# Group-norm statistics of y: small VectorE operations with one operand in PSUM, copies behind them, slot zero's a step later

## The reference, cut to what matters

```python
# x, ctx: (8, 512, 2048); Wt, Wp, Wg: (512, 512); Wz: (512, 64), 8 groups of 64 channels
q = layernorm(x)
t = Wt @ ctx; p = Wp @ q; g = Wg @ ctx              # per batch element
att = sum over (64 channels, 2048) of p * g          # one number per group
y = Wz_group @ (att * t)                             # per group
mu, var = mean and variance of y over (64 channels, 2048), per group
yn = (y - mu) * rsqrt(var + 1e-5)
x = x + (yn * gn_w + gn_b + ctx)
x = x + FFN(layernorm(x))     # 16 heads of 128 features, permuted: up 128x512, gelu, down 512x128
```

## Time and profile before

| what | us |
|---|---|
| median of 3 runs (lowest, highest) | 1515.17 (1512.41, 1517.02) |
| the profiled execution's own time | 1520.61 |
| its span, first to last instruction | 1518.8 |
| TensorE busy in it | 1496.8 |
| VectorE, ScalarE, GpSimd busy | 1201.1, 1065.3, 967.8 |
| granted TensorE clock | 1.00 of full speed |

### The profile page before, as it was taken

One profiled execution on the slowest core, in us unless ns is written; L12 is line 12 of the kernel. 1 busy time (PEld: TensorE's weight loads), 2 busy tenths in 40 slices (PEclk: granted clock), 3 DMA queues, 4 the chain that ended last, 5 costly groups with the idle time before them and its releaser, 6 DMA issues.

```text
span 1518.8 us, 19146 instructions
## 1 busy us (share of the span) xinstructions
PE 1496.8 (99%) x6592; PEld 1231.6 (81%) x6592; DVE 1201.1 (79%) x1514; ACT 1065.3 (70%) x1321; POOL 967.8 (64%) x765
## 2 busy tenths in 40 slices
PE   8999999999999999999999999999999999999998
PEld 7878887887878888888888888888888888877786
DVE  4999868887778767887778877887678876889786
ACT  4636757855778568784687847877478783899786
POOL 1673685298862668525794357835589264888787
PEclk9999999999999999999999999999999999999999
DMA  9998797786667937778376774767748676758886
GB/s 330 329 375 332 230 312 281 270 267 210 226 238 267 286 110 223 253 256 266 125 250 243 250 248 140 266 240 249 215 151 281 250 235 186 259 193 261 272 275 223
DMA packets 166865, 374.76 MB, mean 247 GB/s; under 512 B 14960, under 2 KB 80496, under 8 KB 158576
## 3 DMA queue, kind: packets, MB, share of 16 engines
q1 hardware_dynamic: 141424, 281.25, 56.3%
q0 software_dynamic: 25344, 92.29, 17.1%
HBM read 287.45 MB, written 86.03 MB: 246 GB/s over the span
## 4 chain that ended last, share of the span: by engine, by line
PE 69%; POOL 7%; DVE 7%; DMA 6%; ACT 5%; issue 4%; SPq 1%; POOLq 0%; ACTq 0%; DVEq 0%
PE PP L965 11%; PE PP L950 11%; PE PP L904 11%; PE PP L969 6%; PE PP L953 5%; PE PP L908 5%; PE PP L891 5%; PE PP L892 5%; PE PP L886 5%; PE PP L921 3%; PE PP L925 2%; DVE R L1096 2%; DMA WW<-w_scratch 1%; ACT Z L1043 1%; DMA FB<-xg_scratch,perm_sb 1%
## 5 line engine op out<-in xcount | busy, mean ns | idle before, releaser
L950 PE MATMUL PP<-GG,WW 128*128 128x512 f32 x1008 | 270.0, 390 | 1.0 <-DMA WW<-w_scratch 1.0
L1058 ACT ACTIVATE PP<-PP 128x1024 f32<-128x1024 f32 x256 | 262.1, 1024 | 0.0
L1261 DVE TENSOR_TENSOR R<-PP,R 128x1024 fp32r<-128x1024 f32 x175 | 213.6, 1220 | 55.0 <-ACT PP L1058 54.6
L904 PE MATMUL PP<-R,WC 128*128 128x512 f32 x1024 | 253.2, 389 | 0.2 <-ACT Z L1010 0.2
L1342 POOL TENSOR_TENSOR X<-X,RAW 128x512 f32<-128x512 f32 x112 | 192.5, 1753 | 95.3 <-DVE bn L1081 68.8
L1057 ACT ACTIVATE R<-PP 128x1024 fp32r<-128x1024 f32 x175 | 179.9, 1028 | 90.3 <-PE PP L953 90.0
L1096 DVE TENSOR_TENSOR R<-RAW,R 128x1024 fp32r<-128x1024 f32 x128 | 187.1, 1468 | 49.2 <-ACT R L988 49.2
L904 PEld LDWEIGHTS PP<-R,WC 128*128 128x128 f32 x1024 | 192.2, 188 | 40.6 <-ACT Z L1010 0.7
L950 PEld LDWEIGHTS PP<-GG,WW 128*128 128x128 f32 x1008 | 189.2, 188 | 41.3 <-issue 1.4
L1358 POOL DMA_INDIRECT out<-FB,perm_sb x128 | 150.7, 1177 | 83.0 <-DVE FB L1267 64.5
L891 PE MATMUL PP<-R 128*128 128x512 f32 x512 | 200.0, 391 | 0.2 <-DVE R L1096 0.2
(11 more groups left out here) (122 smaller groups left out, 2586.8 us busy)
## 6 DMA issues: line engine op xcount, KB each, us to landing
WW<-w_scratch SPq DMA_DIRECT2D x148, 512.0 KB, 5.2
X<-in_x SPq DMA_DIRECT2D x32, 1024.0 KB, 5.4
RAW<-in_cx SPq DMA_DIRECT2D x32, 1024.0 KB, 6.4
RAW<-in_xT SPq DMA_DIRECT2D x63, 512.0 KB, 5.7
RAW<-in_cT SPq DMA_DIRECT2D x63, 512.0 KB, 6.8
xg_scratch<-FB SPq DMA_DIRECT2D x104, 256.0 KB, 4.9
w_scratch<-WW POOLq DMA_DIRECT2D x16, 1024.0 KB, 6.8
HX<-wp_scratch SPq DMA_DIRECT2D x7, 1024.0 KB, 8.1
```

The source lines that it names most:

```text
L904: eng.matmul(PP[2 + ot // 2][:, ot % 2, :], WC[:, l, ct, part(ot)], u[:, ct, :], start=(l == 0 and ct == 0), stop=False)
L950: eng.matmul(pp[:, e, :], wt[:, l, part(2 * p + e)], g[:, 0, :], start=(l == 0), stop=False)
L1058: eng.activation(pp[:], pp[:], ACT.Gelu).then_inc(S["gelu"], 1)
L1261: eng.tensor_tensor(h_tile(f, p, 1), PP[slot["up", f, p]][:], f32(h_tile(f, p, 0)), ALU.subtract).then_inc(S["hlo"], 1)
```

## The change

The copy of the means is gone (`bn_aggr` writes mean and variance into `am`, now three rows of four). Of the four chained operations of `g_mean` three remain chained; the difference is computed twice, once into PSUM and once into SBUF, and each operation of the chain has one operand in PSUM. The copy of the PSUM columns, att times 64, and a new att squared go to a new stage `g_copy` behind the second small matmul, ahead of `g_var_a`, which is one operation now instead of two. In slots 1 to 7 `g_mean` moves from 1.25 to 1.18, and so ahead of `h_lo(F, 1)`. In slot 0 everything from `g_var_mm` on moves by 1.0, with the x1 pieces, `load_x(1, ...)`, the squares, `sum_sq`, `root_x1`, `shift_x1`, `turn_sd`, `store_sd` and `xln2`; `turn` and `store_x` stay. One product, `s_hh(1, 0, 3)`, moves from 0.24 to 0.7.

```diff
     def aggr_y(i):
         free["mvy", i] = take(("mvy",))
-        for ot in range(NT + 1):
+        free["att", i] = take(("att",))
+        for ot in range(NT):
             n.up("mvy", i, ot)
...
     def v_att(i, ot):
         if ot == 0:
-            free["att", i] = take(("att",))
+            free["sums", i] = take(("att",))
...
     def g_mean(i):
-        for what in ("gm", "diff", "square", "sum", "att"):
-            t = n.up("gst", i, what)
+        for what in ("diff", "diff2", "square", "sum"):
+            n.up("gst", i, what)
         order.append(("g_mean", i))
+
+    def g_copy(i):
+        for what in ("gm", "att", "att2"):
+            n.up("gst", i, what)
+        order.append(("g_copy", i))
...
-                put(s0 + (dt + 0.08 * c1 if whole else S_EARLY[c1 // 2][dt][c1 % 2]), s_hh, i, dt, c1)
+                put(s0 + (0.7 if (i, dt, c1) == (1, 0, NT - 1) else dt + 0.08 * c1 if whole else S_EARLY[c1 // 2][dt][c1 % 2]), s_hh, i, dt, c1)
...
         put(f0 + 1.2, g_mean_mm, i)
-        put(f0 + 1.25, g_mean, i)
-        put(f0 + 2.3, g_var_mm, i)
-        put(f0 + 2.35, g_var_a, i)
-        put(f0 + 2.4, g_root, i)
-        put(f0 + (3.9 if first else 5.25), g_var_b, i)
+        put(f0 + 1.18, g_mean, i)
+        put(f0 + (3.3 if first else 2.3), g_var_mm, i)
+        put(f0 + (3.33 if first else 2.33), g_copy, i)
+        put(f0 + (3.35 if first else 2.35), g_var_a, i)
+        put(f0 + (3.4 if first else 2.4), g_root, i)
+        put(f0 + (4.9 if first else 5.25), g_var_b, i)
...
-            t = f0 + 5 + 0.8 * k if first else f0 + 3.25 + 2 * (k + 2) if last else base[i + 1] - 0.3 + 0.95 * k
+            t = f0 + 6 + 0.8 * k if first else f0 + 3.25 + 2 * (k + 2) if last else base[i + 1] - 0.3 + 0.95 * k
             put(t, x1_piece, i, ct, hf)
             put(t + (1.2 if last else 0.9), square_x1, i, ct, hf)
             if hf and not last:
                 put(t + 0.1, load_x, i + 1, ct)
-        put(f0 + (4.1 if first else 5.26), mean_x1, i)
-        e = f0 + 12 if first else f0 + 22.8 if last else base[i + 1] + 8.6
+        put(f0 + (5.1 if first else 5.26), mean_x1, i)
+        e = f0 + 13 if first else f0 + 22.8 if last else base[i + 1] + 8.6
...
-                eng.matmul(g_bank(i)[:, 0:8], avg[:], am[:].rearrange("p a b -> p (a b)"), start=True,
+                eng.matmul(g_bank(i)[:, 0:8], avg[:], am[:, 0:2, :].rearrange("p a b -> p (a b)"), start=True,
...
                 for ot in range(NT):
-                    eng.bn_aggr(mvy[:, ot, :], bny[:, ot, :]).then_inc(S["mvy"], 1)
-                dve.wait_ge(*at["mvy", i, NT - 1])
...
-                eng.tensor_copy(am[:, 1, :], mvy[:, :, 0]).then_inc(S["mvy"], 1)
+                    eng.bn_aggr(am[:, 1:3, ot], bny[:, ot, :]).then_inc(S["mvy"], 1)
...
                 dve.wait_ge(*at["gmm", i, 0])
-                eng.tensor_copy(gm[:].rearrange("p a b -> p (a b)"), g_bank(i)[:, 0:8]).then_inc(gst, 1)
-                dve.wait_ge(*at["gst", i, "gm"])
-                eng.tensor_tensor(sm[:, 0, :], am[:, 1, :], gm[:, 1, :], ALU.subtract).then_inc(gst, 1)
-                dve.wait_ge(*at["gst", i, "diff"])
-                eng.tensor_tensor(sm[:, 1, :], sm[:, 0, :], sm[:, 0, :], ALU.mult).then_inc(gst, 1)
+                diff, square = g_bank(i)[:, 12:16], g_bank(i)[:, 16:20]
+                eng.tensor_tensor(diff, am[:, 1, :], g_bank(i)[:, 4:8], ALU.subtract).then_inc(gst, 1)
+                eng.tensor_tensor(sm[:, 0, :], am[:, 1, :], g_bank(i)[:, 4:8], ALU.subtract).then_inc(gst, 1)
+                dve.wait_ge(*at["gst", i, "diff2"])
+                eng.tensor_tensor(square, diff, sm[:, 0, :], ALU.mult).then_inc(gst, 1)
                 dve.wait_ge(*at["gst", i, "square"])
-                eng.tensor_tensor(sm[:, 2, :], sm[:, 1, :], mvy[:, :, 1], ALU.add).then_inc(gst, 1)
-                eng.tensor_scalar(sm[:, 3, :], gm[:, 0, :], 64.0, None, ALU.mult).then_inc(gst, 1)
-            elif stage == "g_var_a":
+                eng.tensor_tensor(sm[:, 2, :], square, am[:, 2, :], ALU.add).then_inc(gst, 1)
+            elif stage == "g_copy":
                 i = a[0]
                 gst = S["gst"]
                 dve.wait_ge(*at["gmm", i, 1])
+                eng.tensor_copy(gm[:].rearrange("p a b -> p (a b)"), g_bank(i)[:, 0:8]).then_inc(gst, 1)
+                eng.tensor_scalar(sm[:, 3, :], g_bank(i)[:, 0:4], 64.0, None, ALU.mult).then_inc(gst, 1)
                 dve.wait_ge(*at["gst", i, "att"])
-                eng.tensor_tensor(sm[:, 4, :], g_bank(i)[:, 8:12], sm[:, 3, :], ALU.mult).then_inc(gst, 1)
-                dve.wait_ge(*at["gst", i, "va"])
-                eng.tensor_tensor(sm[:, 4, :], sm[:, 4, :], sm[:, 3, :], ALU.mult).then_inc(gst, 1)
+                eng.scalar_tensor_tensor(out=sm[:, 4, :], in0=g_bank(i)[:, 0:4], scalar=64.0, in1=sm[:, 3, :],
+                                         op0=ALU.mult, op1=ALU.mult).then_inc(gst, 1)
+            elif stage == "g_var_a":
+                i = a[0]
+                gst = S["gst"]
+                dve.wait_ge(*at["gmm", i, 1])
+                dve.wait_ge(*at["gst", i, "att2"])
+                eng.tensor_tensor(sm[:, 1, :], g_bank(i)[:, 8:12], sm[:, 4, :], ALU.mult).then_inc(gst, 1)
...
-                pool.wait_ge(*at["gst", i, "vaa"])
-                eng.tensor_scalar(ve[:, 2, :], sm[:, 4, :], EPS, None, ALU.add).then_inc(S["gpw"], 1)
+                pool.wait_ge(*at["gst", i, "va"])
+                eng.tensor_scalar(ve[:, 2, :], sm[:, 1, :], EPS, None, ALU.add).then_inc(S["gpw"], 1)
```

More of the change, by code:

```diff
@@ L310, in g_var_a @@
         give(n.up("gst", i, "va"), ("PP", *g_bank(i)))
-        n.up("gst", i, "vaa")
         order.append(("g_var_a", i))
@@ L786, in build_in @@
     mv1 = sb("mv1", [P, NT, 2])
-    mvy = sb("mvy", [P, NT, 2])
     sq = sb("sq", [P, NT, 2])
@@ L801, in build_in @@
     sd = cold[:, 0:2 * NT].rearrange("p (k t) -> p k t", k=2)
-    am = sb("am", [P, 2, NT])
+    am = sb("am", [P, 3, NT])
     gm = sb("gm", [P, 2, NT])
@@ L932, in tensor @@
                 pe.wait_ge(*at["avg", 2])
-                pe.wait_ge(*at["mvy", i, NT])
+                pe.wait_ge(*at["mvy", i, NT - 1])
                 pe.wait_ge(*at["att", i, NT - 1])
-                eng.matmul(g_bank(i)[:, 0:8], avg[:], am[:].rearrange("p a b -> p (a b)"), start=True,
+                eng.matmul(g_bank(i)[:, 0:8], avg[:], am[:, 0:2, :].rearrange("p a b -> p (a b)"), start=True,
                            stop=True).then_inc(S["gmm"], 1)
@@ L1149, in vector @@
                     dve.wait_ge(*t)
-                for ot in range(NT):
-                    eng.bn_aggr(mvy[:, ot, :], bny[:, ot, :]).then_inc(S["mvy"], 1)
-                dve.wait_ge(*at["mvy", i, NT - 1])
                 for t in free["att", i]:
                     dve.wait_ge(*t)
-                eng.tensor_copy(am[:, 1, :], mvy[:, :, 0]).then_inc(S["mvy"], 1)
+                for ot in range(NT):
+                    eng.bn_aggr(am[:, 1:3, ot], bny[:, ot, :]).then_inc(S["mvy"], 1)
             elif stage == "v_att":
@@ L1160, in vector @@
                 if ot == 0:
-                    for t in free["att", i]:
+                    for t in free["sums", i]:
                         dve.wait_ge(*t)
@@ L1169, in vector @@
                 dve.wait_ge(*at["gmm", i, 0])
-                eng.tensor_copy(gm[:].rearrange("p a b -> p (a b)"), g_bank(i)[:, 0:8]).then_inc(gst, 1)
-                dve.wait_ge(*at["gst", i, "gm"])
-                eng.tensor_tensor(sm[:, 0, :], am[:, 1, :], gm[:, 1, :], ALU.subtract).then_inc(gst, 1)
-                dve.wait_ge(*at["gst", i, "diff"])
-                eng.tensor_tensor(sm[:, 1, :], sm[:, 0, :], sm[:, 0, :], ALU.mult).then_inc(gst, 1)
-                dve.wait_ge(*at["gst", i, "square"])
-                eng.tensor_tensor(sm[:, 2, :], sm[:, 1, :], mvy[:, :, 1], ALU.add).then_inc(gst, 1)
-                eng.tensor_scalar(sm[:, 3, :], gm[:, 0, :], 64.0, None, ALU.mult).then_inc(gst, 1)
+                diff, square = g_bank(i)[:, 12:16], g_bank(i)[:, 16:20]
[3 more added lines that the diff above has]
+                eng.tensor_tensor(square, diff, sm[:, 0, :], ALU.mult).then_inc(gst, 1)
+                dve.wait_ge(*at["gst", i, "square"])
+                eng.tensor_tensor(sm[:, 2, :], square, am[:, 2, :], ALU.add).then_inc(gst, 1)
[3 more added lines that the diff above has]
+                dve.wait_ge(*at["gmm", i, 1])
+                eng.tensor_copy(gm[:].rearrange("p a b -> p (a b)"), g_bank(i)[:, 0:8]).then_inc(gst, 1)
+                eng.tensor_scalar(sm[:, 3, :], g_bank(i)[:, 0:4], 64.0, None, ALU.mult).then_inc(gst, 1)
+                dve.wait_ge(*at["gst", i, "att"])
+                eng.scalar_tensor_tensor(out=sm[:, 4, :], in0=g_bank(i)[:, 0:4], scalar=64.0, in1=sm[:, 3, :],
+                                         op0=ALU.mult, op1=ALU.mult).then_inc(gst, 1)
             elif stage == "g_var_a":
@@ L1181, in vector @@
                 dve.wait_ge(*at["gmm", i, 1])
```

(8 more changed lines are left out.)

## The result

| | before | after |
|---|---|---|
| median of 12 runs, us (lowest, highest) | 1515.57 (1512.41, 1517.60) | 1521.34 (1517.94, 1526.14) |
| profiled execution, own time / span, us | 1520.61 / 1518.8 | 1520.57 / 1518.8 |

The ratio is 1.0038, 95% interval 1.0028 to 1.0047: **the kernel is slower by 5.8 us** (4.2 to 7.1). The two profiled executions took equally long. That of before lies 5 us above its median, that of after does not. So the spans can't be compared, only stretches of them, counted from a mark close to the change.

The account below looks back on a forecast made before the run. TensorE, busy 1496.8 of 1518.8 us, was taken as the bound. Slot 1's +3.8 and slot 2's +0.4 gave +4.2 on the median 1515.17: 1519.4 us, own range 1517.5 to 1520.5, whole range 1511.5 to 1521.8.

Parts of the forecast that it names:

- The delay of `shift_x1`: Slot 0's pieces a unit later: shift_x1 starts later by 2.3 to 4.6 us, taken as 4.0.
- The walk: VectorE's queue in slot 0, added up by durations: 2.8 us idle before s_lo(1, 12), shift_x1 later by 4.5 us.
- Later by the delay less 0.2.: Slot 1: y_mm(1, 2, 0) starts later by shift_x1's delay less 0.2 us, slack 0.18 us; +3.8 us.
- The 0.8 us saved in slot 0 are swallowed.: Slot 0: shorter TensorE waits save 0.8 us with restarts, but none of it remains at y_mm(1, 2, 0).
- Slots 1 and 3 to 7: The later bank release for dn_mm and the moved g_mean cost 0; in slots 3 to 7, 0.9 us to spare.
- Slot 2: The bank release for dn_mm comes 0.46 us later, with nothing to spare; +0.4 us, bounds +0.5 and -2.4.
- PSUM operands: VectorE's small operations: no surcharge by the rows, 151 to 158 ns with PSUM against 161 to 164 without.
- Rival A: TensorE's statistics waits go and nothing else comes: 3.0 us plus restarts or only 0.8 gained, 1511.9 to 1514.4; chance 0.22.
- Rival B: Clearly slower: data for s_lo(1, 12) land later, passing one for one to y_mm(1, 2, 0); 1521.9 with 2.5 us more; chance 0.16.
- The data of step 12: The transfer s_lo(1, 12) needs in slot 0, issued behind load_x(1, 0); it cannot start before some 141.1.
- Rival C: Stalls come to PSUM forms or the next s_lo, and slot 1 has unseen slack: nothing changes, 1515.2; chance 0.10.

Follow-up runs that it names:

- sum step only: The kernel before with only sum_sq, root_x1, shift_x1 and xln2 of slot 0 a step later, the x1 pieces unmoved; ratio 1.0031 to the kernel before.
- pieces back: The changed kernel with only slot 0's x1 pieces, what follows them and mean_x1 back at their old times; ratio 0.9986 to the kernel before.
- both moves: The changed kernel with y_lo(1, 0) put behind shift_x1 and load_s(1, 6) ahead of load_x(1, 0); ratio 0.9995 to the kernel before.
- load_s first: The changed kernel with load_s(1, 6) put ahead of load_x(1, 0) in SyncE's queue; ratio 1.0043 to the kernel before.
- Forms alone: The changed kernel, its new small operations kept, with all of slot 0's plan times as before; ratio 1.0001 to the kernel before.

## Why the prediction was right, and where its sizes were off

- *Direction and place.* The forecast was +4.2 us and 1519.4; measured +5.8 and 1521.34. That is inside the whole range (1511.5 to 1521.8), but above the forecast's own of 1517.5 to 1520.5; 0.4 of it is the median of before, 1515.57 for 1515.17. The place, the line from `shift_x1` over `load_c(1, 3)` to `y_mm(1, 2, 0)`, and the two waits (predicted near 168 and 180 with 4 to 5 us; they began at 167.8 and 183.9 and took 4.45) are shown by the profile, and by sum step only, pieces back and both moves.
- *The delay of `shift_x1`*, term +4.0: **this is the term that was mis-sized.** Measured 5.0. The walk itself gave 4.5; I took less. Of the walk, the idle time before `s_lo(1, 12)` was 2.85 (I had 2.8), and from there to `shift_x1` 14.0 (I had 14.1). Wrong was that `g_var_b` would start at the same time, because GpSimd was held by its own weight work. It started at 128.90, and 0.6 us later counted from `s_hh(1, 0, 0)`. The weight work was over 1.9 us earlier than before, so counted (its last issue ended at 124.95, and at 125.27 before). But `g_copy` now stood behind two `s_lo` in VectorE's queue, which took 5.43 us together (119.72) where I had 1.15 each, so GpSimd waited 0.84 us for `g_var_a`. Then its own two operations took 1.12 and 1.87 us where they had taken 0.27 and 1.05, with two `s_lo` running on VectorE beside them (125.61 to 127.96). Started 1.0 us earlier, they took 1.7 longer: that is the 0.6. An `s_lo` has both inputs in SBUF; that VectorE and GpSimd held each other up here is inferred from the times, as for the `s_lo` of 3.02 us at 122.46 before.
- *"Later by the delay less 0.2."* Measured 5.3 for a delay of 5.0. Of the 0.18 us between `y_ev` and `y_mm` 0.06 stayed, so the slack was 0.1; and `load_c(1, 3)` took 0.5 us longer. Over thirteen of the fourteen profiles `y_mm(1, 2, 0)` began 27.4 to 28.1 us behind `shift_x1`; the one apart is load_s first.
- *The 0.8 us saved in slot 0 are swallowed.* Right: TensorE was 1.2 us early up to the first wait (`y_mm(1, 0, 2)` began at 162.22 and, before, at 161.93, which is 49.4 and 50.7 us from `s_hh(1, 0, 0)`), and none of it was left after it. Pieces back keeps 0.8 of it up to `y_mm(1, 3, 0)`.
- *The clock* was not in the prediction. In the changed kernel, by the line above, it did not change the sum: TensorE still came 1.22 us too early for the bank of `y_mm(1, 2, 0)`. In sum step only it was 1.7 of 4.7 us.
- *Slots 1 and 3 to 7*, 0. Right: no wait for L1194 there. In slot 3 it ended at 555.53, and `dn_mm` started at 556.52: 1.0 us to spare, I had 0.9.
- *Slot 2*, +0.4. From the gather's issue to `dn_mm` it was 10.43 us before and 10.89 after (360.02 to 370.91): the 0.46 are there. But from the first small matmul to that `dn_mm` it was 8.72 us before and 7.01 after: the gather came earlier in respect to TensorE. The wait for the bank should have grown beyond 0.9; it was 0.91, and 0.8 to 2.0 in the other kernels with the new forms and the gather in its old place. So the sign of this term is open. Forms alone, where it stands with the other gains of the forms, is 1.0001, which allows -1.2 to +1.4 us.
- *PSUM operands.* By rows, no surcharge. Right: 146 to 171 ns, against 161 to 164 before with all operands in SBUF and nothing in the way; the three chained operations took 0.62 us as forecast. I passed over the 219 to 224 ns of L1185, a small stall in every slot and not the operation's own length. The rule of the Trainium skill ("VectorE: DVE Perf Modes", section on the TRN2 errata) has a fixed 120 cycles for a source in PSUM against 58 in SBUF, by estimate 65 ns more; the trace does not agree with it, for operations of four and eight columns.
- *Rival A* (the stalls go, nothing else comes) fell: the time rose. Even without slot 0's times, in forms alone, its 3 us did not come. *Rival B* was there in part. The data of step 12 took as long as before from issue to landing (7.05 us, 135.16 to 142.21; before 7.04), but the issue itself was 0.6 us later counted from `s_hh(1, 0, 0)`: it waits behind `load_x(1, 0)`, that for the second x1 piece, and that for `g_var_b`. These 0.6 us went through to `shift_x1` one for one, as B says; they and the 0.5 us by which I took less than the walk are the mis-sized part. B's 2.5 us of a slower landing did not come. *Rival C* fell in its time, though an `s_lo` behind the sum did take 2.10 us (119.72, beside a GpSimd operation from 119.70).

## What to carry to other kernels

Moving a stage later in a hand-written order moves it behind everything in the interval, on every queue. Walk each queue with the durations of the trace before calling a step free: here `sum_sq` to `xln2`, a few small operations and one `y_lo` further back, cost 3.0 us through a buffer and a transfer, and 1.7 more by the clock. Ask what the last link's slack is (0.1 us here); it says whether a gain upstream can arrive, and whether a delay will. And judge parts of a fix together, since two that give nothing alone can give all together, as here.
